# Layer 0's sums of squares as two fp16 halves, and layer 0's steps in another order

## The reference, cut

```python
h = relu(hypergraph_conv(x, adj, W1, b1))     # 512 hidden features
h = layer_norm(h, gamma, beta)                # needs the mean and the variance of h
y = hypergraph_conv(h, adj, W2, b2) + x
x = _layernorm(x + y)
# hypergraph_conv(x): D^-1 H B^-1 H^T (x @ W^T) + b, H = (adj != 0),
# B from column counts, D from row sums weighted with adj's first row
```

## Time and profile before

| | us |
|---|---|
| median of 3 runs | 736.91 (736.59 to 742.61) |
| the profiled execution | 737.08 |
| its span | 735.2 |
| TensorE busy | 676.4 (92%) |
| VectorE busy | 554.1 (75%) |
| ScalarE busy | 529.9 (72%) |
| GpSimd busy | 343.5 (47%) |

### The profile page before, as it was taken

One profiled execution on the slowest core, in us unless ns is written; L12 is line 12 of the kernel. 1 busy time (PEld: TensorE's weight loads), 2 busy tenths in 40 slices (PEclk: granted clock), 3 DMA queues, 4 the chain that ended last, 5 costly groups with the idle time before them and its releaser, 6 DMA issues.

```text
span 735.2 us, 17541 instructions
## 1 busy us (share of the span) xinstructions
PE 676.4 (92%) x5654; PEld 494.2 (67%) x5654; DVE 554.1 (75%) x1744; ACT 529.9 (72%) x1177; POOL 343.5 (47%) x418
## 2 busy tenths in 40 slices
PE   5999999999999997698998799999999998999995
PEld 4667777777777775355555566666666666877874
DVE  3888888878887866278888687876778784676765
ACT  4667788777777767267887677667776777788875
POOL 2233354444444336155666335243343444766763
PEclk9999999999999999799999799999999999999998
DMA  9423232222222103066765244454344443475673
GB/s 278 134 72 95 77 114 74 73 74 73 71 71 71 58 1 58 29 159 129 134 136 118 45 89 85 89 87 76 79 93 81 94 66 65 96 165 138 156 164 120
DMA packets 168168, 71.42 MB, mean 97 GB/s; under 512 B 122260, under 2 KB 165654, under 8 KB 168088
## 3 DMA queue, kind: packets, MB, share of 16 engines
q1 hardware_dynamic: 166496, 70.41, 40.7%
q10 hardware_dynamic: 1592, 0.01, 0.1%
HBM read 28.46 MB, written 8.39 MB: 50 GB/s over the span
## 4 chain that ended last, share of the span: by engine, by line
PE 36%; DMA 11%; SPq 3%; DVE 3%; issue 2%; POOL 1%; ACT 1%; ACTq 0%; POOLq 0%; DVEq 0%
PE bank L110 11%; DMA xT_lo<-x_halves 11%; PE bank L112 10%; PE bank L111 10%; SPq L1139 3%; PE bank L1213 1%; PE bank L1412 1%; POOL x_halves L1125 1%; DVE l_st L1039 1%; PE bank L1518 1%; DVE l_pre L1288 1%; PE bank L1225 1%; ACT l_mid_hi L1572 0%; DVE l_lr L1652 0%; PE bank L1809 0%
## 5 line engine op out<-in xcount | busy, mean ns | idle before, releaser
L1073 ACT ACTIVATE x_resident<-l_pre,l_nmr,l_rstd 128x256 f32<-128x256 f32 (+1 forms) x256 | 137.1, 598 | 16.6 <-POOL l_nmr L1067 16.6
L1125 POOL TENSOR_TENSOR x_halves<-x_resident,x_halves 128x1024 f16<-128x1024 f32 x46 | 100.9, 2193 | 38.0 <-DVE l_pre L1288 28.0
L1039 DVE BATCH_NORM_STATS2 l_st<-l_pre 128x6 f32<-128x256 f32 x256 | 96.5, 414 | 1.1
L110 PE MATMUL bank<-Wk_lo,xT_hi 128*128 128x2 f16 (+2 forms) x384 | 93.9, 274 | 3.3 <-DMA xT_lo<-x_halves 3.1
L111 PE MATMUL bank<-Wk_hi,xT_lo 128*128 128x2 f16 (+2 forms) x384 | 95.0, 273 | 0.0
L112 PE MATMUL bank<-Wk_hi,xT_hi 128*128 128x2 f16 (+2 forms) x384 | 94.7, 272 | 0.0
L983 POOL TENSOR_TENSOR hq<-hq 128x512 f32<-128x512 f32 x32 | 43.1, 1348 | 77.1 <-ACT hq L716 77.1
L1064 POOL TENSOR_TENSOR l_rstd<-l_veps,minus_half 128x4 f32<-128x4 f32 x64 | 64.6, 1009 | 20.4 <-DVE l_veps L1053 17.2
L110 PE MATMUL bank<-W2T_lo,h_hi 128*128 128x257 f16 x256 | 70.7, 276 | 2.3 <-DVE h_lo L860 1.2
L112 PE MATMUL bank<-W2T_hi,h_hi 128*128 128x257 f16 x256 | 70.9, 277 | 0.0
L111 PE MATMUL bank<-W2T_hi,h_lo 128*128 128x257 f16 x256 | 70.9, 277 | 0.0
(11 more groups left out here) (206 smaller groups left out, 2067.9 us busy)
## 6 DMA issues: line engine op xcount, KB each, us to landing
adj<-in_adj SPq DMA_DIRECT2D x32, 256.0 KB, 3.8
x_halves<-in_x SPq DMA_DIRECT2D x16, 512.0 KB, 4.0
x_resident<-in_x SPq DMA_DIRECT2D x16, 512.0 KB, 5.1
out<-x_resident SPq DMA_DIRECT2D x15, 512.0 KB, 3.2
l_adjT<-adjT_resident SPq DMA_DIRECT2D x16, 256.0 KB, 2.6
x_resident<-in_L_gnn_W SPq DMA_DIRECT2D x2, 512.0 KB, 5.6
x_resident<-in_L_gnn_Wk SPq DMA_DIRECT2D x1, 768.0 KB, 8.1
xT_hi<-x_halves SPq DMA_TRANSPOSE x48, 3.2
```

What stands on the lines that cost most here:

```text
L110: nc.tensor.matmul(out, lhs[0], rhs[1], start=start, stop=False, **kw)
L1039: dve.bn_stats(L.st[p][:, j, :], L.pre[p][:, j, :]).then_inc(L.st_ok, 1)
L1073: act.activation(K.x[:, gcols(g, j)], L.pre[p][:, j, :], ACT.Identity, bias=L.nmr[p][:, j:j + 1], scale=L.rstd[p][:, j:j + 1]).then_inc(L. ...
L1125: pool.tensor_tensor(F.xs[p][1], x_group(K, g), F.xs[p][0], ALU.subtract).then_inc(F.x_lo, 1)
```

## The change

The squares are scaled by 0.25 (`SQ_SCALE` 0.5 inside the square), and the variance's factor takes that back. `hqs` becomes two fp16 tiles: `squares_high` on ScalarE copies the sum, `squares_low` on GpSimd subtracts the copy from the sum. `square_sums` makes two fp16 products of one column where it made one in fp32, and waits for both halves. All three sums now write in place in `hq`. The lists of all engines but SP are reordered, and TensorE's last step goes, since `mix_z` moves from the beginning of a step to the end of the one before. The diff, its indentation cut:

```diff
+SQ_SCALE = 0.5
...
+hq, hqs = sb("hq", [128, HT, C]), halves("hqs", [128, C])
...
     if j == 0:
-        pe.wait_ge(hqs_ok, upto(g, 3, 3))
-    pe.matmul(b_z[j % 2][:, D + 1:D + 2], hqs[:, j * N:(j + 1) * N], K.ones[:, 0:1],
-              start=True, stop=True).then_inc(z_ps, 1)
+        pe.wait_ge(sq_hi, upto(g, 1, 1))
+        pe.wait_ge(sq_lo, upto(g, 1, 1))
+    o, c = b_z[j % 2][:, D + 1:D + 2], slice(j * N, (j + 1) * N)
+    pe.matmul(o, hqs[1][:, c], K.ones16[:, 0:1], start=True, stop=False)
+    pe.matmul(o, hqs[0][:, c], K.ones16[:, 0:1], start=False, stop=True).then_inc(z_ps, 1)
...
 def step(g, p, has):
     q = 1 - p
-    if has(-2):
-        mix_z(g - 2, p, 0)
-        mix_z(g - 2, p, 1)
+    if has(1):
+        transpose_adj(g + 1, q)
     if has(0):
         gram(g, p)
     if has(-1):
         project(g - 1, 0)
-    if has(1):
-        transpose_adj(g + 1, q)
+    if has(0):
+        mix_x(g, p, 0)
+        mix_x(g, p, 1)
     if has(-1):
         project(g - 1, 1)
+        square_sums(g - 1, 0)
+    if has(1):
+        degree(g + 1, q)
     once(g, 1, W.turn_qkv, pe)
-    if has(0):
-        mix_x(g, p, 0)
-    if has(-1):
-        square_sums(g - 1, 0)
-        square_sums(g - 1, 1)
-    if has(0):
-        mix_x(g, p, 1)
     once(g, 0, W.fold, pe)
     if has(-1):
+        square_sums(g - 1, 1)
         project(g - 1, 2)
-    if has(1):
-        degree(g + 1, q)
-    if has(-1):
         square_sums(g - 1, 2)
         project(g - 1, 3)
         square_sums(g - 1, 3)
...
+    once(g, -1, W.turn_w12, pe)
     if has(0):
         hidden(g, p, 0)
         hidden(g, p, 1)
     if has(1):
         spread_degrees(g + 1, q)
-    once(g, -1, W.turn_w12, pe)
     if has(0):
         hidden(g, p, 2)
         hidden(g, p, 3)
-over_groups(pe, step, 1, 2)
+    if has(-1):
+        mix_z(g - 1, q, 0)
+        mix_z(g - 1, q, 1)
+over_groups(pe, step, 1, 1)
...
-    act.activation(hq[:, h, :], hf[:, h, :], ACT.Square).then_inc(h_sq, 1)
+        if h == 0:
+            act.wait_ge(sq_lo, upto(g - 1, 1, 1))
+    act.activation(hq[:, h, :], hf[:, h, :], ACT.Square, scale=SQ_SCALE).then_inc(h_sq, 1)
...
+def squares_high(g):
+    act.wait_ge(hqs_ok, upto(g, 3, 3))
+    if reused(g, 1):
+        act.wait_ge(z_ps, upto(g - 1, GP, GP))
+    act.activation(hqs[0][:], hq[:, 0, :], ACT.Copy).then_inc(sq_hi, 1)
...
-    if has(-1):
-        copy_z(g - 1, 0)
     if has(0):
         mixed_high(g, p, 0)
-    if has(-1):
-        copy_z(g - 1, 1)
-    if has(0):
         mixed_high(g, p, 1)
     once(g, 0, W.high_w2, act)
     once(g, 0, W.high_rows, act)
+    if has(-1):
+        copy_z(g - 1, 0)
+        copy_z(g - 1, 1)
     once(g, 1, W.high_qkv, act)
+    if has(-1):
+        copy_z(g - 1, 2)
     once(g, 2, W.scale_w3, act)
     once(g, 2, W.scale_wk, act, 0)
     once(g, 3, W.scale_wk, act, 1)
     once(g, 3, W.scale_wk, act, 2)
     once(g, 4, W.high_w3, act)
-    once(g, 5, W.high_wk, act, 0)
-    once(g, 6, W.high_wk, act, 1)
     if has(-1):
-        copy_z(g - 1, 2)
         copy_z(g - 1, 3)
+    if has(-2):
+        norm_apply(K, L, act, g - 2, p, 0)
+        norm_apply(K, L, act, g - 2, p, 1)
     if has(0):
         hidden(g, 0)
         hidden(g, 1)
+    once(g, 5, W.high_wk, act, 0)
+    once(g, 6, W.high_wk, act, 1)
+    once(g, -1, W.high_w1, act)
+    if has(0):
         square(g, 0)
         hidden(g, 2)
+    if has(1):
+        copy_degrees(g + 1)
+    if has(0):
         square(g, 1)
         hidden(g, 3)
         square(g, 2)
-    if has(1):
-        copy_degrees(g + 1)
-    once(g, -1, W.high_w1, act)
-    once(g, -1, W.scale_w2, act)
+    if has(-2):
+        norm_apply(K, L, act, g - 2, p, 2)
     if has(0):
         square(g, 3)
+    once(g, -1, W.scale_w2, act)
     if isinstance(g, int) and g == G - 1:
         first_high(0)
         first_high(1)
-    if has(-2):
-        norm_apply(K, L, act, g - 2, p, 0)
-        norm_apply(K, L, act, g - 2, p, 1)
     if has(2):
         copy_adj(g + 2)
+    if has(0):
+        squares_high(g)
     if has(-2):
-        norm_apply(K, L, act, g - 2, p, 2)
         norm_apply(K, L, act, g - 2, p, 3)
 over_groups(act, step, 2, 2)
...
+    dve.scalar_tensor_tensor(zvar[:], zf[:, :, D + 1], W_SCALE / (H * SQ_SCALE * SQ_SCALE), zm2[:], ALU.mult,
...
     q = 1 - p
-    if has(-1):
-        normalise(g - 1, q, 0)
-    if has(0):
-        hidden_low(g, 0)
-        hidden_low(g, 1)
-    if has(-1):
-        normalise(g - 1, q, 1)
-        normalise(g - 1, q, 2)
-        normalise(g - 1, q, 3)
+    if has(1):
+        scale_incidence(g + 1, q, 1)
     if has(0):
         hidden_low(g, 2)
-        hidden_low(g, 3)
+    once(g, -1, W.low_w1, dve)
     if has(-1):
         layer_out(g - 1, q, 0)
-        norm_row(L, dve, g - 1, q, 0, 2)
+    if has(0):
+        hidden_low(g, 3)
     if has(1):
         operator(g + 1, q)
-    once(g, -1, W.low_w1, dve)
+    if has(-1):
+        norm_row(L, dve, g - 1, q, 0, 2)
+        norm_row(L, dve, g - 1, q, 1, 2)
+    once(g, 0, W.products, dve, 0)
     if has(-1):
         layer_out(g - 1, q, 1)
-        norm_row(L, dve, g - 1, q, 1, 2)
         norm_row(L, dve, g - 1, q, 2, 2)
-        norm_row(L, dve, g - 1, q, 3, 2)
-    once(g, 0, W.products, dve, 0)
     once(g, 0, W.products, dve, 1)
     once(g, 1, W.products, dve, 2)
+    if has(2):
+        incidence(g + 2, p)
     once(g, 1, W.products, dve, 3)
+    if has(2):
+        edge_weights(g + 2)
     once(g, 2, W.score_sums, dve, 0)
+    if has(-1):
+        norm_row(L, dve, g - 1, q, 3, 2)
     once(g, 2, W.score_sums, dve, 1)
     once(g, 3, W.score_sums, dve, 2)
     once(g, 3, W.score_sums, dve, 3)
-    once(g, 3, W.score_columns, dve)
-    if has(2):
-        incidence(g + 2, p)
-        edge_weights(g + 2)
+    if has(1):
+        mixed_low(g + 1, q, 0)
     if has(-1):
         norm_variance(L, dve, g - 1, q, 0.25 * EPS)
     if has(1):
-        mixed_low(g + 1, q, 0)
         mixed_low(g + 1, q, 1)
+    once(g, 3, W.score_columns, dve)
     once(g, -1, W.centre_w2, dve)
     if has(2):
-        counts(g + 2, p)
         degrees(g + 2)
     once(g, -1, W.low_w2, dve)
     once(g, 0, W.low_qkv, dve)
@@ -958,8 +968,17 @@
     if has(0):
         hidden_norm(g)
     if has(2):
+        counts(g + 2, p)
+    if has(0):
+        normalise(g, p, 0)
+        normalise(g, p, 1)
+        normalise(g, p, 2)
+        normalise(g, p, 3)
+    if has(1):
+        hidden_low(g + 1, 0)
+        hidden_low(g + 1, 1)
+    if has(2):
         scale_incidence(g + 2, p, 0)
-        scale_incidence(g + 2, p, 1)
...
+    pool.tensor_tensor(hq[:, 0, :], hq[:, 0, :], hq[:, h, :], ALU.add).then_inc(hqs_ok, 1)
+
+def squares_low(g):
+    pool.wait_ge(sq_hi, upto(g, 1, 1))
+    pool.wait_ge(hqs_ok, upto(g, 3, 3))
+    if reused(g, 1):
         pool.wait_ge(z_ps, upto(g - 1, GP, GP))
-    pool.tensor_tensor((hqs if h == HT - 1 else hq[:, 0, :])[:], hq[:, 0, :], hq[:, h, :],
-                       ALU.add).then_inc(hqs_ok, 1)
+    pool.tensor_tensor(hqs[1][:], hq[:, 0, :], hqs[0][:], ALU.subtract).then_inc(sq_lo, 1)
...
     if isinstance(g, int) and g == G - 2:
         first_low(0)
         first_low(1)
-    once(g, -2, W.constants, pool)
-    once(g, -2, W.sum_rows, pool)
     if has(0):
         norm_scales(K, L, pool, g, p)
     if has(1):
         hidden_power(g + 1)
+    once(g, -2, W.constants, pool)
+    once(g, -2, W.sum_rows, pool)
     if has(2):
         sum_squares(g + 2, 1)
         sum_squares(g + 2, 2)
         sum_squares(g + 2, 3)
     once(g, 2, W.low_w3, pool)
+    if has(2):
+        squares_low(g + 2)
     once(g, 3, W.low_wk, pool, 0)
```

More of the change, by code:

```diff
@@ L508, in layer0 @@
         hs = halves("h", [128, HT, C])
-        hq, hqs = sb("hq", [128, HT, C]), sb("hqs", [128, C])
+        hq, hqs = sb("hq", [128, HT, C]), halves("hqs", [128, C])
         zf, zn = sb("zf", [128, GP, D + 2]), [sb(f"zn{p}", [128, GP, D]) for p in range(2)]
@@ L521, in layer0 @@
             sem, ("hid_ps", "hf_ok", "h_hi", "h_sq", "h_lo", "hqs_ok"))
+        sq_hi, sq_lo = map(sem, ("sq_hi", "sq_lo"))
         z_ps, zf_ok, zvar_ok, zrs_ok, zn_ok = map(sem, ("z_ps", "zf_ok", "zvar_ok", "zrs_ok", "zn_ok"))
@@ L891, in hidden_norm @@
                     dve.wait_ge(zvar_ok, upto(g, 3, 1))
-                    dve.scalar_tensor_tensor(zvar[:], zf[:, :, D + 1], W_SCALE / H, zm2[:], ALU.mult,
+                    dve.scalar_tensor_tensor(zvar[:], zf[:, :, D + 1], W_SCALE / (H * SQ_SCALE * SQ_SCALE), zm2[:], ALU.mult,
                                              ALU.subtract).then_inc(zvar_ok, 1)
@@ L980, in sum_squares @@
                         pool.wait_ge(hqs_ok, upto(g, 3, h - 1))
-                    elif reused(g, 1):
+                    pool.tensor_tensor(hq[:, 0, :], hq[:, 0, :], hq[:, h, :], ALU.add).then_inc(hqs_ok, 1)
[3 more added lines that the diff above has]
+                    if reused(g, 1):
                         pool.wait_ge(z_ps, upto(g - 1, GP, GP))
```

(3 more changed lines are left out.)

## The result

The changed kernel is slower. Its median is 745.91 us (741.88 to 751.31, 4 runs) against 736.96 us of the kernel before on the same chip, a ratio of 1.013 (95% interval 1.008 to 1.018). Run again later (`after_again`) it gave 745.29 us and 1.011 (1.006 to 1.016). The profiled execution took 745.84 us with a span of 743.9. That is inside the stated range of 732 to 746 us, at its upper end, and above the 744.3 us up to which the prediction spoke of no change.

What follows compares the result with a forecast made beforehand. TensorE's own list was taken to bound layer 0's steady steps. Start -0.7, one-time pieces +3.1, steady steps -1.0 and end +1.2 summed to +2.6 us: 739.7 us, range 732 to 746.

Steps and rivals of the forecast that it cites:

- the start: Before the steady steps, up to hidden(1,0): a shorter chain to the QKV low half, -0.7 us (0 to -1.5).
- the steady part: Layer 0's steady steps: product saving less the waits, a gain of about 0.07 us each, 1.0 over 14 steps.
- The fp32 products: TensorE's square_sums in each step: 0.74 us becomes 0.20 with fp16 products, so pure issue time falls by 0.54.
- The wait for the copy of z: TensorE ahead of project(2) in each step: 0.67 us from the first pair, 0.37 of it uncovered stall.
- The later low half: TensorE ahead of square_sums: low half late from GpSimd's chain, 0.1 us of stall a step (0 to 0.3).
- `layer_out` at no cost: Second layer_out ahead of the second half of mix_x in each step: covered by 0.1 us only, costed at nothing.
- rival B: Slower: GpSimd's chain later than forecast, deciding from 0.3 us more a step, 749 us at 0.6; chance 0.18.
- One-time pieces: Steps with weight pieces: products 1.0 us, low_w3 0.6, high_wk about 0.75 each of two, +3.1 in all.
- The end: Last group of layer 0: first wait ends about 2.0 us later, project(2) starts 0.9 later; sum +1.2 (0 to 2.5).
- the clock's part: End of layer 0: more of the last two projections at the lower granted clock after longer waits, +0.6 us.
- Layers 1 to 3 at nothing: Everything behind layer 0: no term in the sum, so counted as unchanged.
- Rival C: Faster: neither wait forms in layer 0's steps, 16.23 us a step, 729 us; chance 0.08.

Runs made afterwards that it cites:

- old_low_dve: Lists of the kernel before with the fp16 halves, low half on VectorE, second half of mix_x split around the first two square_sums: 740.1 us, ratio 1.008.
- after_low_dve: Changed kernel with squares_low moved from GpSimd to VectorE, behind incidence: 739.5 us, ratio 1.006.
- once_back: Changed kernel with high_wk, low_w3 and the last two products moved to where their engine idles or nobody waits: 744.2 us, ratio 1.009.
- after_last32: Changed kernel with TensorE taking the last group's sums of squares from the fp32 sum again: 750.5 us, ratio 1.018.
- before_longer: Kernel before with gram's products issued twice in layer 0: 746.4 us, ratio 1.013.
- low_dve_once: old_low_dve with the one-time weight pieces on VectorE and GpSimd moved off the low half's chain: 738.5 us, ratio 1.003.
- low_dve_best: low_dve_once with the last group's sums in fp32, and low_w3 and low_wk behind the sums, waiting for the low half: 734.2 us, ratio 1.000.

## Why the prediction was right or wrong

**The sign of the sum was right, its size was not.** The forecast was +2.6 us; the medians differ by 8.9 and 8.5. In the trace layer 0 accounts for 4.7 (304.32 to 309.06), in which the start gave back 1.2 where I had 0.7. The third `gram` begins anywhere from 47.0 to 50.4 us over all the traces (before 47.2 and 47.7, changed kernel 47.0 and 47.8), so that term, -0.7, can be neither confirmed nor refuted. Steps and end together are +5.9, where the forecast had 3.1 - 1.0 + 1.2 = 3.3. Of the 6.1 us between forecast and trace, the steady part of the steps made 2.9, the end 0.9 and layers 1 to 3, taken at nothing, 4.0; the one-time pieces (-1.2) and the start (-0.5) went the other way. So two steps failed, the steady part and the term left at nothing. That the time still fell into the range is owed to its width.

**The fp32 products: right.** The pairs stand 0.05 us apart. old_low_dve shows what is left when nothing waits: 16.77 - 16.37 = 0.40 a step of the 0.54.

**The wait for the copy of z: right.** Forecast 0.67 from pair to `project(2)`, measured 0.66, in every trace of the changed kernel.

**The later low half: the mis-sized term.** I took 0.1 us a step, 0 to 0.3 with the bounds. It is 0.17 where the steps are unrolled: the chain ends 0.08 later than I had it (5.51 behind the old place of `gram`, 5.43 forecast), and TensorE starts 0.15 behind the subtraction and not 0.05. It is 0.37 in the looped steps, where the three sums follow each other at once and take 4.83 us, 1.61 each, and not the 1.28 to 1.38 of the earlier trace rows; the third ends 0.38 later than I had it. The durations of GpSimd that I took from the old list did not hold in the new one, where other VectorE operations lie beside them; that these are the reason is argued, not shown. after_low_dve took this wait away by moving one operation, and its late steps fell by 0.24 unrolled and by 0.16 to 0.47 looped.

**`layer_out` at no cost: wrong.** I had called the second half of `mix_x` covered by 0.1 us only and then put in nothing. It costs 0.1 a step unrolled and 0.2 looped. A cover of 0.1 us in a chain of estimates is half a cost.

The three together: forecast 16.70, measured 16.88 unrolled and 16.98 to 17.18 looped. Times 13, the steady part is about +2 and not -1, and that is the first step of the prediction that failed; the other is that layers 1 to 3 stood at nothing. It is rival B in its mechanism (the GpSimd chain later than I have it), at about a half of the size where I let it decide.

**One-time pieces: right in kind, too large.** Forecast 3.1, measured 1.93 (once_back). The `products` cost 0.46 and not 1.0 (17.34 against 16.88, with the wait for `wcol_lo` at 53.05), `low_w3` 0.54 where I had 0.6, `high_wk` 0.54 a time and not 0.75. Where the rest went was not tested.

**The end: right in its first links, too small.** The waits for the sum and for the copy are 2.49 and 0.42 (forecast: 2.0 more for the first, none to speak of for the second). But the first pair starts 3.4 us later than before, counted from the old place of `gram` (22.5 against 19.1), and not 2.0: the fp32 sum itself is ready 1.3 later (20.33 against 19.05), which I had left out. `project(2)` starts 2.3 later and not 0.9. In the first trace the clock's part was +0.7 from there to the end of the last `square_sums` (5.4 us against 4.7), forecast 0.6, and what follows gave back 0.9, forecast 0.3. Sum +2.1 in place of +1.2. In after_again, the same program, the `project` took 4.5 us, no more than before, what follows gave back 0.3, and the sum was +1.9. So that the forecast of the clock's part came out in the first trace is luck.

**Layers 1 to 3 at nothing: wrong.** I took them for a constant. They took 434.8 and 431.8 us in two traces of one program, 430.9 in two of the kernel before, and 434.5 in a kernel whose only difference was a longer layer 0. In the executions of any one kernel the span goes with the mean granted clock, by about 0.55 us longer for each 0.001 less (a fit over some 160 executions of all these comparisons; the kernel before alone spreads over 11 us of span). On the chip of after_again the mean spans of the changed kernel and the kernel before differ by 8.0 us. Steps and end make 5.8 of it in that kernel's trace, the lower mean clock (0.9755 against 0.9773) 1.0, and 1.2 remain, about the size of one more wait on DMA.

A later layer 0 is not the whole reason. The medians of all the kernels lie 2.0 to 4.7 us further above the kernel before than their steps and their end account for (after_last32: 8.5), or 1.5 to 5.2 by the ratios on record: 3.0 and 2.8 for the changed kernel's two sets, 4.7 for before_longer, but also 4.3 and 2.1 for old_low_dve and low_dve_once, whose layer 1 starts within 1.1 us of the first trace of the kernel before, and 3.6 for low_dve_best, whose layer 1 starts 4 us early. By the fit a lower mean clock covers 4.1 of old_low_dve's 4.3, but none of before_longer's 4.7. The rest of this term stays open: no run here separates the start of the kernel, which varies by 3 us and of which each kernel has one trace, from DMA waits and clock.

**Rival C (faster, 729)** needed both waits to be absent. With the lists of the change they can't be; with lists made for it the step came to 16.33, and the layer to 4.3 us less, of which the median shows about 1.5, not to be told from nothing. That is no test of C's time: the missing 3 us are the open term above.

## What to carry to other kernels

Cheaper products on the bounding engine bought nothing here, because their operands come from a chain that had no slack. Cost the chain first, then place the new operations where that chain ends earliest, which here was VectorE and not the idler GpSimd. Idle time of GpSimd is free only where VectorE idles too, reads a PSUM bank, or runs something that nobody waits for. And a term that is "just covered" by 0.1 us, fifteen times over, belongs into the sum with half its size. Last, give the part that the change does not touch a range of its own: here it moved by 4.0 us in the first trace, where layer 0 moved by 4.7.
